# Folding the bias and the decay factor of Q into one VectorE instruction, in an eight-core attention and feed-forward kernel

## The reference, cut to what is computed

```python
k = x @ Wk.T + bk ; v = x @ Wv.T + bv ; q = x @ Wq.T + bq      # M = 128 columns each
def step(state, kvq):                                          # along the sequence
    out_t = einsum('bij,bj->bi', state, q_t)
    state = 0.99 * state + 0.01 * einsum('bi,bj->bij', v_t, k_t)
y = outs @ Wo.T + bo
x = x + layernorm(attn(layernorm(x)))
h = silu(x @ wg.T) * (x @ wu.T)                                # HIDDEN = 3072
x = x + layernorm(ffn(layernorm(x)))
```

## The kernel before, in words

| steps | what | engine |
|---|---|---|
| 1-2 | load x | SP |
| 3-20 | statistics for the first norm | ACT, DVE |
| 21-37 | reciprocal root, 17 small ones | DVE |
| 38-39 | `xhat` (L313) | DVE |
| 40-43 | eight transposes into a bank (L322), copy to `x1T` (L326), for lb 0 and 1 | PE, DVE |
| 44, 45, 46 | Q matmuls into bank 4 (L335), `qt` from bank 4 (L343), `qt` times `lamq` (L346) | PE, ACT, DVE |
| 47, 48 | K matmuls into bank 5, `kt` (L350) | PE, ACT |
| 49, 50 | V matmuls into bank 4, `vt` (L354) | PE, ACT |
| 51-54 | transposes of kt (L358) and vt (L361), lb 0; the same, lb 1 | PE |
| 55-58 | `khat` (L365) and `vtm` (L368), lb 0; the same, lb 1 | DVE, ACT |
| 59-64 | lb 0: kt times qt into bank 5 (L374); `pwt` from it (L377); two matmuls into bank 4 (L383, L386); `ot` (L390); `khat` times `vtm` into bank 5 (L392); state update of three DVE instructions (L398, L400 reads bank 5, L402) | |
| 65-70 | the same for lb 1 | |
| 71 | the four matmuls of `y1mm` for lb 0, into banks 4 and 5 (L410, L414) | PE |
| 72-96 | statistics, 17 small steps, `mr` (L288), `apply2` (L424, two L429 that read banks 4 and 5), statistics of X | DVE |
| 97-122 | the same 26 steps for lb 1, its `y1mm` being 97 | |
| 123-141 | 17 small steps, `xhat` (L440) twice | DVE |

## Time and profile before

### The profile page before, as it was taken

How to read it: one execution, slowest core, us unless ns; L and a number is a source line. 1 busy time by engine, 2 the same in 40 slices (tenths; PEclk the granted TensorE clock), 3 DMA queues, 4 the chain that set the end, 5 groups by cost and what they waited for, 6 DMA issues and landing times.

```text
span 2712.3 us, 53391 instructions; the slowest of 8 cores (2705.0 to 2712.3 us)
## 1 busy us (share of the span) xinstructions
PE 2355.0 (87%) x17792; PEld 1687.5 (62%) x17792; DVE 1621.3 (60%) x5570; ACT 614.4 (23%) x1633; POOL 62.9 (2%) x85
## 2 busy tenths in 40 slices
PE   1879889889889889889889889889898898898897
PEld 0556666666666666666666666666666666666665
DVE  4545676565675565665566665665665656755653
ACT  1222122222122222122222122221222221222211
POOL 3410000000000000000000000000000000000000
PEclk8989999999999999999999999999999999999999
DMA  9960000000000000000000000000000000000000
GB/s 140 139 74 24 32 32 32 32 1 32 32 32 32 32 1 32 32 32 32 32 1 32 32 32 32 24 9 32 32 33 32 11 23 32 32 32 32 1 17 32
DMA packets 76414, 90.60 MB, mean 33 GB/s; under 512 B 56432, under 2 KB 56560, under 8 KB 76144
## 3 DMA queue, kind: packets, MB, share of 16 engines
q0 software_dynamic: 57136, 20.06, 7.1%
q1 hardware_dynamic: 19008, 67.12, 6.9%
HBM read 73.67 MB, written 33.55 MB: 40 GB/s over the span
## 4 chain that ended last, share of the span: by engine, by line
PE 45%; DVE 25%; issue 10%; DVEq 7%; DMA 6%; ACT 5%; ACTq 2%; POOL 0%; POOLq 0%
PE pb L537 14%; PE pb L548 13%; PE pb L527 12%; DVEq L656 7%; DVE hT L557 5%; PE pb L335 3%; DVE X L429 2%; DVE ui L238 2%; ACT x1T L259 2%; DMA wu_sb<-wub 2%; DVE tt L236 2%; DVE tt L235 2%; ACTq L656 2%; ACT x1T L263 2%; PE pb L322 2%
## 5 line engine op out<-in xcount | busy, mean ns | idle before, releaser
L548 PE MATMUL pb<-x3T,wu_sb 128*128 128x256 bf16 x6144 | 803.6, 274 | 126.2 <-DVE hT L557 115.1
L537 PE MATMUL pb<-x3T,wg_sb 128*128 128x256 bf16 x6144 | 820.5, 278 | 53.9 <-DVE x3T L515 35.2
L527 PE MATMUL pb<-wd_sb,hT 128*128 128x512 bf16 x3072 | 787.3, 381 | 0.0
L537 PEld LDWEIGHTS pb<-x3T,wg_sb 128*128 128x128 bf16 x6144 | 599.5, 100 | 269.2 <-issue 85.8
L548 PEld LDWEIGHTS pb<-x3T,wu_sb 128*128 128x128 bf16 x6144 | 583.5, 98 | 243.0 <-issue 174.9
L542 ACT ACTIVATE hT<-pb 128x256 bf16<-128x256 f32 x768 | 293.8, 383 | 1765.7 <-PE pb L537 1663.8
L557 DVE TENSOR_TENSOR hT<-hT,pb 128x256 bf16<-128x256 bf16 x768 | 322.1, 419 | 542.6 <-PE pb L548 534.7
L527 PEld LDWEIGHTS pb<-wd_sb,hT 128*128 128x128 bf16 x3072 | 300.4, 98 | 209.2 <-issue 11.8
L322 PE MATMUL pb<-identb,xhat 128*128 128x128 bf16 x512 | 55.8, 275 | 112.5 <-DVE xhat L313 112.5
L322 PEld LDWEIGHTS pb<-identb,xhat 128*128 128x128 bf16 x512 | 47.3, 128 | 130.3 <-issue 126.9
L429 DVE SCALAR_TENSOR_TENSOR X<-pb,rr,X 128x512 f32<-128x512 f32 x128 | 96.1, 751 | 11.1 <-issue 0.4
(11 more groups left out here) (79 smaller groups left out, 1401.1 us busy)
## 6 DMA issues: line engine op xcount, KB each, us to landing
X<-x SPq DMA_DIRECT2D x64, 512.0 KB, 3.7
out<-X SPq DMA_DIRECT2D x64, 512.0 KB, 2.9
wg_sb<-wgb POOLq DMA_DIRECT2D x24, 256.0 KB, 13.9
wu_sb<-wub POOLq DMA_DIRECT2D x24, 256.0 KB, 15.2
wd_sb<-wdb POOLq DMA_DIRECT2D x24, 256.0 KB, 14.9
wq_sb<-wqT POOLq DMA_DIRECT2D x1, 256.0 KB, 12.0
wk_sb<-wkT POOLq DMA_DIRECT2D x1, 256.0 KB, 19.8
wv_sb<-wvT POOLq DMA_DIRECT2D x1, 256.0 KB, 24.2
```

The source lines that it names most:

```text
L527: mm(lambda E, j=j, jp=jp, lb=lb, dh=dh, dbk=dbk: E.matmul(bank[dbk][:], hT[:, jp * 256 + lb * 128: jp * 256 + (lb + 1) * 128], wd_sb[:, j ...
L537: mm(lambda E, j=j, dc=dc: E.matmul(bank[2][:, 0:256], wg_sb[:, j * 1024 + dc * 128: j * 1024 + (dc + 1) * 128], x3T[:, dc * 256:(dc + 1) ...
L548: mm(lambda E, j=j, dc=dc: E.matmul(bank[3][:, 0:256], wu_sb[:, j * 1024 + dc * 128: j * 1024 + (dc + 1) * 128], x3T[:, dc * 256:(dc + 1) ...
```

## The change

The ACT instruction that adds the bias while it copies bank 4 to `qt`, and the DVE instruction that multiplies `qt` by `lamq` in place, become one DVE instruction that reads bank 4, adds the bias per partition, multiplies by `lamq` and writes `qt`. The list of stage A has one step less.

```diff
             A.append(proj(wq_sb, ("wq",), 4))
-            A.append(lambda: P.emit("act", lambda E: E.activation(
-                qt[:], bank[4][:, 0:GPB * C], AF.Identity, bias=bq_s[:]),
-                reads=(("bank", 4), ("bq",)), writes=(("qt",),)))
-            A.append(lambda: P.emit("dve", lambda E: E.tensor_tensor(
-                qt[:], qt[:], lamq[:], ALU.mult),
-                reads=(("qt",), ("lamq",)), writes=(("qt",),)))
+            A.append(lambda: P.emit("dve", lambda E: E.scalar_tensor_tensor(
+                qt[:], bank[4][:, 0:GPB * C], bq_s[:], lamq[:], ALU.add, ALU.mult),
+                reads=(("bank", 4), ("bq",), ("lamq",)), writes=(("qt",),)))
             A.append(proj(wk_sb, ("wk",), 5))
```

## The result

The changed kernel takes 2772.5 us in the median of its runs against 2716.6, a ratio of 1.0206 with a 95% interval of 1.0193 to 1.0218: 56 us slower. The forecast was slower by 32 us, 2746, with 2718 to 2772 as its range. The sign is right, the loss is 1.75 times the forecast one, and the time lies at the very edge, just outside. Whether the loss is over 2% the interval leaves open. The profiled execution of after has a span of 2769.2 us on its slowest core.

A forecast was written before the change was run, and what follows sets the result against it. The prediction took PE, 87% busy, as the bound, so its standing still counts. Its terms, 1.15 + 0.70 - 0.81 + 0 = 1.04 us a tile, times 31 gave 32 us on 2713.8: 2746 us, range 2718 to 2772.

The forecast's parts named there:

- The instructions themselves: Removed and added qt instructions: DVE gets 4.5 us more, ACT 15 less, both vanishing in idle engine time.
- (1): At j = 6 the new instruction stands ahead of the product, making it later: cost 0, up to 0.2 us.
- (2): Slot a of j = 7: PE stands still 1.15 us a tile before the transpose of vt, 1.25 at most.
- (3): At j = 8 the kt-qt product of lb 1, directly behind the state product of lb 0, waits: +0.70 us.
- (4): The wait at L383 goes, as the gate matmuls now lie between L374 and L383: -0.81 us a tile.
- (5): j = 12 to 20, y1mm of lb 1 ahead of the gate matmuls: between -0.2 and +0.36 us, taken as 0.
- The sum: All terms for a tile: 1.04 us, times 31 is 32 us; bounds 0.48 to 1.76 us a tile.
- The clock: Falls of the granted clock: same count as before, priced at 0.75 to 1.14 us a tile in either direction.
- slower by over 2%: Rival: a second half-clock stretch in every tile, at j = 17, 1.14 us each, 2781 us; chance 0.20.
- No cost at all: Rival: PE's other rhythm avoids the half-clock stretch at L322, giving back 0.75 of 1.04 us, 2723 us; chance 0.15.
- Faster: Rival: faster by over 2%, needing two freed handovers on PE's path, at least 1.75 us a tile; chance 0.02.
- the edit only does what it says: Rival: the steps' places do not matter and DVE's and ACT's changes are hidden, 2714 us; no separate chance given.

The follow-up runs named there:

- e8: The kernel before with eight empty steps ahead of the transposes of xhat, plus the fused instruction with one empty step ahead of it; ratio 1.0069.
- e1: The changed kernel with one empty step ahead of the fused instruction, so that all places are the old ones; 2829.8 us, ratio 1.0421.
- e2: The changed kernel with one empty step behind the fused instruction, so that all later steps have their old places; ratio 1.0234, which is 2780 us.
- e6: The changed kernel with an empty step ahead of the first transpose of vt, putting it and all later steps in their old places; 2768.1 us, ratio 1.0185.
- e5: The kernel before with the eight gate matmuls of j = 8 issued twice, between the two long waits; ratio 1.0143, 39 us more.
- e4: The kernel before with the eight gate matmuls of j = 22 issued twice, behind both long waits; ratio 1.0034, 9 us more.
- e3: The kernel before with its two qt instructions (ACT, then DVE) kept but taken as one step, nothing fused; 2784.5 us, ratio 1.0254.

## Why the prediction was right and wrong

*The instructions themselves.* I took 0.42 us for the new instruction, and its mean is 0.484, a little above my upper bound of 0.474. This changes nothing: it is hidden, as e8 shows. The Trainium skill ("VectorE: DVE Perf Modes", "Specifications") places ScalarE closer to PSUM. The durations hardly differ (0.484 against 0.474); the price that e1 found is a queue's.

*(1) Cost 0 by cover.* Right, and only by cover: e2 and e6 take the cover away and find 0.9 us a tile.

*(2) The wait for vt, 1.15.* Right: 0.99 idle in the row above, and from where PE was ready (0.06 behind the start of the transpose of kt, 1709.23) to 1710.44 it is 1.15.

*(3) +0.70 and (4) -0.81.* Right: 0.54 idle, the 0.76 of tile 0 again, and the wait at L380 gone.

*(5) 0.* Right within its bounds: L407 waits 0.61 and 0.15, and up at j = 14 no longer waits. In the tile of the rows it is 23.97 us from the gate matmuls of j = 10 to the up matmuls of j = 17, against 24.01 before.

*The sum.* 1.04 a tile. Tiles without a fall are 0.99 longer, with the first fall 1.22, with both 1.34; at equal numbers 1.20. So the sum of the waits held for tiles at full clock. The 0.16 above it (5 us in all) are in tiles where a part of the matmuls runs at the lower clock; which of the terms grows there I didn't measure.

*The clock: the step that failed.* The prediction said "I take the same count as before". The count went from 0.92 to 1.42 falls a tile, worth 0.60 us a tile or 19 of the 24 us that were missing. The rival "slower by over 2%" named the place (j = 17) and a price of 1.14 for the second stretch; measured, both falls against the first alone cost 84.48 - 83.29 = 1.19. It said "in every tile", and it came in 55% of them. I gave it a chance of 0.20 because there was one case in 31. That argument was weak: in the kernel before 24 of 232 tiles had no fall and 203 exactly one, 189 of them at the same wait. A number that regular suggests the spacing of the waits rather than each wait by itself, and the edit changed the spacing, from 40.70 to 41.87 us. The price of the first fall was low too: I took 0.75 from one tile, and over all tiles of before it is 82.07 - 80.93 = 1.14. My own sign of being wrong, a clock share that moves by more than 0.02, could not catch this: one fall more in every tile moves it by 0.02 (0.98 to 0.96), and the half fall more that came moved it by 0.01, from 0.972 to 0.962. The Trainium skill ("TensorE: Matmul & The Clock Gate", "Why this matters for your kernels") warns of idle gaps between matmul bursts, above a length that the two long waits of a tile do not reach here. The traces go further: the stand at L322 is 2.6 us in the timeline of a tile, and 194 of the 232 tiles of before have a fall there; and e5 has the second fall in 86 tiles, against 19, with no idle gap added, so the placing of the old gaps is enough.

*The other rivals.* "No cost at all" assumed fewer falls; e4 shows that this happens (0.39), but for work behind both waits. "Faster" and "the edit only does what it says" are out: e3 has the whole loss with nothing fused.

## What to carry to other kernels

Where steps are threaded into a loop by count, removing one moves all that follow, and the moves have to be priced before the instruction is: write the list of slots before and after, and look for each step that loses the work between it and its producer. Fusing a bank's evacuation into an engine's second pass was free here only where nothing long stood ahead of it on that engine; look at what holds the bank, not at the durations. And a wait that costs nothing under another wait has a price the moment the other is mended.

## What the runs showed of the hardware that I had not expected

The same 0.87 us of matmuls costs 9 us in one place and 39 in another of the same kernel, and in the changed kernel about 40 (tiles of 85.07 us against 83.75, times 31), all over 32 tiles. Most of the difference is the number of stretches at the lower granted clock: a first one costs 1.14 us in a tile of before and 1.37 in one of after. In this kernel, with two waits of over 2 us per tile, a comparison within 1% between two versions therefore says little about the edit unless tiles with the same number of falls are compared.
